# Eight-layer graph network on one core: the sum-stage loops of four engines and TensorE's product loop are loaded at the first slot of an instruction fetch block

## The reference

```python
def layer(h, params):
    W, b, g, beta = params
    h = h * norm_out
    agg = jax.ops.segment_sum(h[src], dst, num_segments=n)
    agg = agg * norm_in
    out = agg @ W + b
    out = _layer_norm(out, g, beta)
    out = jax.nn.gelu(out, approximate=False)
    return (out, None)
h, _ = jax.lax.scan(layer, features, (Ws, bs, ln_g, ln_b))
...
x = _layernorm(x + _L0_gnn_ref(x, src, dst, Ws, bs, ln_g, ln_b), axis=-1)
```

## Time and profile before

| | |
|---|---|
| median of 3 runs | 1668.79 us (1665.58 to 1670.16) |
| the profiled execution's own time | 1669.91 us |
| its span from first to last instruction | 1668.2 us |
| granted TensorE clock, mean share | 0.808 |
| rounds of the sum loop over the 8 layers | 32 (3, 3, 3, 3, 3, 4, 5, 8) |
| rounds of PE's product loop | 84 (7, 7, 7, 7, 9, 11, 14, 22) |

### The profile page before, as it was taken

The page is one execution under the profiler, slowest core; times in us unless marked ns, Lnnn a source line. Parts: engine busy times, 40 slices in busy tenths (PEclk is TensorE's granted clock), DMA queues, the critical chain, the costliest instruction groups (busy, mean ns, idle before and its releaser), DMA issues.

```text
span 1668.2 us, 29286 instructions
## 1 busy us (share of the span) xinstructions
PE 1110.4 (67%) x6235; PEld 916.9 (55%) x6235; DVE 880.2 (53%) x2153; ACT 528.1 (32%) x853; POOL 846.9 (51%) x1023
## 2 busy tenths in 40 slices
PE   7665378677596695776776696679956769992000
PEld 7444123666575575656656585667846667882000
DVE  6445577245354372463563274326733226776776
ACT  4132230232332332233333232333323333441444
POOL 1554300545445464455455365445745445765886
PEclk9556559788898897798898898789987889996555
DMA  0930000523514415225225324441244448545998
GB/s 14 377 130 3 2 1 6 159 82 126 158 57 139 133 69 170 78 107 163 71 106 164 107 76 138 139 126 66 91 139 147 149 126 321 189 169 180 312 302 291
DMA packets 98038, 224.52 MB, mean 135 GB/s; under 512 B 14496, under 2 KB 14496, under 8 KB 97968
## 3 DMA queue, kind: packets, MB, share of 16 engines
q0 software_dynamic: 34432, 104.72, 21.2%
q1 hardware_dynamic: 57200, 107.52, 17.9%
q10 hardware_dynamic: 6336, 11.54, 1.9%
HBM read 137.91 MB, written 85.82 MB: 134 GB/s over the span
## 4 chain that ended last, share of the span: by engine, by line
PE 53%; issue 12%; DMA 10%; DVE 8%; POOL 5%; ACT 4%; another core or an unknown queue 3%; ACTq 2%; DVEq 2%; POOLq 0%; SPq 0%
PE ps_a L1200 16%; PE ps_y L1220 9%; PE ps_y L1221 9%; PE ps_y L1225 9%; DMA rows<-h_rows,slot 4%; POOL rows L507 3%; DMA rows<-h_rows,idx_f 2%; PE ps_y L1216 2%; DMA h_rows<-rows 2%; PE ps_a L1115 2%; DVE agg_t L607 2%; PE ps_a L1181 1%; ACT agg_t L958 1%; DVEq L821 1%
## 5 line engine op out<-in xcount | busy, mean ns | idle before, releaser
L1200 PE MATMUL ps_a<-sel,rows 128*128 128x128 f32 x2560 | 407.0, 323 | 278.1 <-DVE sel L789 122.8
L1200 PEld LDWEIGHTS ps_a<-sel,rows 128*128 128x128 f32 x2560 | 377.1, 233 | 309.6 <-issue 309.0
L456 POOL DMA_INDIRECT rows<-h_rows,slot x290 | 279.8, 965 | 258.3 <-issue 124.6
L995 ACT ACTIVATE agg_t<-ps_a 128x508 f32 x320 | 190.7, 596 | 520.7 <-PE ps_a L1200 369.8
L464 POOL TENSOR_TENSOR s_lo<-agg_t,s_hi 128x512 fp32r<-128x512 f32 x168 | 216.9, 1293 | 251.3 <-ACT s_hi L1000 251.3
L789 DVE TENSOR_SCALAR sel<-iota,by_tile 128x128 f32<-128x128 f32 x344 | 126.0, 370 | 395.6 <-PE ps_a L1200 207.2
L1220 PE MATMUL ps_y<-w_hi,s_hi 128*128 128x512 f32 x672 | 268.5, 400 | 10.9 <-ACT s_hi L1000 10.8
L1221 PE MATMUL ps_y<-w_lo,s_hi 128*128 128x512 f32 x672 | 267.6, 398 | 0.0
L1225 PE MATMUL ps_y<-w_hi,s_lo 128*128 128x512 f32 x672 | 183.5, 396 | 0.0
L862 DVE BATCH_NORM_STATS2 small<-ps_y 128x6 f32<-128x512 f32 x168 | 117.3, 698 | 96.1 <-PE ps_y L1225 95.9
L1220 PEld LDWEIGHTS ps_y<-w_hi,s_hi 128*128 128x128 f32 x672 | 129.0, 192 | 42.0 <-issue 15.1
(11 more groups left out here) (210 smaller groups left out, 1268.2 us busy)
## 6 DMA issues: line engine op xcount, KB each, us to landing
h_rows<-rows SPq DMA_DIRECT2D x124, 256.0 KB, 2.0
h_rows<-agg_t SPq DMA_DIRECT2D x1, 20480.0 KB
out<-agg_t SPq DMA_DIRECT2D x78, 256.0 KB
agg_t<-in_x SPq DMA_DIRECT2D x19, 1024.0 KB, 5.7
h_rows<-rows ACTq DMA_DIRECT2D x44, 256.0 KB, 2.3
w_raw<-in_Ws SPq DMA_DIRECT2D x32, 256.0 KB
rows<-h_rows,slot POOLq DMA_INDIRECT x290
rows<-in_ln_g SPq DMA_DIRECT2D x8, 256.0 KB, 3.8
```

The costliest lines, as they stand in the source:

```text
L456: g.indirect_dma_start(out=rows[:, k, :], out_offset=None, in_=table[:, :], in_offset=bass.IndirectOffsetOnAxis(ap=slot[:, k:k + 1], axis=0))\
L995: a.activation(agg_t[:, :, bass.ds(r0 + 1, P - 1)], ps_a[k % GS][:, :, 1:P], ACT.Copy)\
L1200: m = mm(ps_a[k % GS][:, b, :], rows[:, k, b * P:(b + 1) * P], sel[:, k % GS, :], start=True, stop=True)
```

## The change

```diff
+ENG = mybir.EngineType
...
+        def paged(engine, start, end):
+
+            return nc.Fori(start, end, engines=(engine,), head_slot={engine: 0})
...
             def sum_stage(L, table, its, ib):
-                with pool.Fori(0, its) as group:
+                with paged(ENG.Pool, 0, its) as group:
...
                 def tiles(first, end):
-                    with dve.Fori(first, end) as group:
+                    with paged(ENG.DVE, first, end) if end is its else dve.Fori(first, end) as group:
...
-                with act.Fori(0, its) as group:
+                with paged(ENG.Activation, 0, its) as group:
...
             def sum_stage(L, its, ib):
-                with pe.Fori(0, its) as group:
+                with paged(ENG.PE, 0, its) as group:
...
                 pe.wait_ge(b_ok, done(L + 1))
                 pe.sem_inc(pe_tick, 1)
-                with pe.Fori(0, pairs) as pair:
+                with paged(ENG.PE, 0, pairs) as pair:
```

## The result

| | before | after |
|---|---|---|
| median of the runs | 1667.90 us (4 runs, 1665.58 to 1670.16) | 1717.07 us (4 runs, 1709.54 to 1722.05) |
| the profiled execution's own time | 1669.91 us | 1718.0 us |
| ratio | | 1.0296, 95% interval 1.0257 to 1.0334 |

The kernel is 49 us slower.

A forecast was written before the change was run, and what follows sets the result against it. PE bounds the product stages, a chain of waits the sum stages. Profiled 1669.9 us plus 34.5 for stops minus 3 gain gave 1701.4; the runs' median, 1.1 lower, gave 1700.3, stated as 1700, range 1664 to 1725.

The forecast's parts named there:

- Where the chain runs: POOL's and DVE's sum-stage loop entries lie in single file with PE's wait, so delays there count fully.
- Blocks of 128, fetched in their order: POOL, DVE, ACT and SP fetch blocks of 128 instructions in order, PE 256; a target behind a skipped block needs fetching.
- Which entries: Stops at POOL's and DVE's loop entries of layers 1 to 7, 7 each, plus one in layer 0: 15.
- one of the two of layer 0: Allowance of one stop for POOL's and DVE's first entries, which depend on runtime code outside the program.
- The price of a stop: Each on-demand fetch at POOL's or DVE's loop entry stops the engine for 2.3 us.
- the 15 stops: All stops at POOL's and DVE's loop entries: 15 x 2.3 = 34.5 us lost.
- The 4 KB load: The bias load, 2.28 us from issue to DVE's first use, taken as the measure for one stop.
- The upper bound of 3.8: A stop at POOL's or DVE's entry costs at most 3.8 us, as SP's loads of 256 KB.
- What to look for in the profile: POOL's landing-to-gather wait about 3.7 us, DVE's bias-to-selection wait about 3.5, PE's longest wait for rows 13.8.
- The gain of 3 us: DVE's and ACT's loop bodies inside one block save boundary crossings in about half of 32 rounds: about 3 us.
- The lower bound, 0: Least gain from DVE's and ACT's loop bodies lying inside one block: 0 us; the upper bound was 11 us.
- PE and ACT at no cost: PE's and ACT's loop heads lie in the next block and crossings hide behind waits: cost 0.

The follow-up runs named there:

- e4_blocks_of_128: Changed kernel with POOL's, DVE's and ACT's loops placed by multiples of 128 instead of 256, so no block is skipped: 1690.66 us, 1.0074 of the kernel before.
- e7_dve_early: Kernel before, with only DVE's jump to a multiple of 256 added, ahead of its wait for the bias: 1521.28 us, ratio 1.0003.
- e10_dve_two_jumps: Kernel before, with two DVE jumps to multiples of 256, an empty instruction between, ahead of its third-piece loop: 1737.63 us, ratio 1.0339.
- e3_act_pe_only: Kernel before, with only ACT's sum loop and PE's two loops placed as in the change: 1685.05 us, ratio 1.0019.
- e8_both_early: Kernel before, with POOL's jump ahead of its waits for stored rows and DVE's ahead of its bias wait: 1521.05 us, ratio 1.0007.
- e6_pool_two_stops: Kernel before, with two alignments and a semaphore increment between them ahead of POOL's gather loop; only one branch resulted: 1543.53 us, ratio 1.0155.
- e9_two_stops_apart: Kernel before, with two POOL jumps to multiples of 256, an empty instruction between, ahead of its gather loop: 1725.88 us, ratio 1.0264.

## Why the prediction was right

**Where the chain runs.** Right. Both entries stand in single file with PE's wait: the stops cost nothing that can be measured when a wait covers them, and about their full length when none does.

**Blocks of 128, fetched in their order.** Right, and now shown. POOL stops where a block of 128 is skipped, and doesn't where none is (e4_blocks_of_128). The packets fit a fetch in order, in which the block jumped over is brought as well: DVE's 362 instructions a layer take 2.83 blocks without placement, and with it three and the one that is jumped over, so 8 x 1.17 = 9 more, as measured (59 against 50). A second jump adds two blocks in each of 8 layers, 16 more, as measured (75). The stops, and the packet inside each of the 14, show that the block behind the one jumped over had not come yet. The prediction held that the trace shows how many packets came and not which; their times, which it left aside, settle it. The queues are told apart as it assumed: the 16.4 KB packets rose only where PE's loops were placed. PE's blocks are of 256 instructions (16,384 bytes), those of POOL, DVE and ACT of 128 (8,192 bytes).

**Which entries.** POOL's and DVE's of layers 1 to 7, and one of the two of layer 0: right to the count. For layer 0 that was luck, since one of two was an allowance without a reason. The one is POOL's (3.71 us); DVE's in layer 0 shows 0.57 us, as much as the entry of the next block in e4_blocks_of_128 (0.54).

**The price of a stop.** This is the term of the sum that was mis-sized: 2.3 us, taken from the bias's landing, where the runs show 2.86 for POOL and 3.36 for DVE (without the jump's own few hundredths, gaps of 2.56 to 3.03 and of 2.97 to 3.47). Over the 15 stops it is 46.9 us, 3.13 each, instead of 34.5. The 4 KB load was a poor stand-in: in the stop of the third layer POOL waits 1.03 us until the packet starts, 0.46 us for the packet, and 1.07 us more before it goes on. The upper bound of 3.8 held for the mean, though single stops go beyond it (4.06 us in e7_dve_early, 5.0 in e10_dve_two_jumps). What to look for in the profile was right in kind, short in size for the same reason: 3.99 us where 3.7 stood, 4.64 where 3.5 stood, 14.9 where 13.8 stood.

**The gain of 3 us.** Not seen. e3_act_pe_only, which has it for ACT, is at 1.0019 and e8_both_early at 1.0007. The lower bound, 0, was the better value. The two errors have the same sign: 12.4 us for the stops and 3 us for the gain make up 15.4 of the 17 us by which the time is over 1700. Counted by the layers alone, which lost 51.5 us, 4 us more are missing; the shorter last part hides them.

**PE and ACT at no cost.** Right within what can be measured: 0 to 0.4%.

## What to carry to other kernels

Before code is aligned, count what the alignment jumps over. On POOL and DVE, whose instructions come in packets of 8.2 KB, a branch over a whole block of 128 instructions stopped the engine for 2.56 to 3.47 us here, and a branch to the next block cost 0.4 to 0.5 us. If code has to be aligned, put the jump ahead of a wait that the engine has anyway and that is longer than the stop, and not between a landing and the work that the critical chain needs. A loop across a block boundary was no loss that could be measured here (ACT's and PE's placed alone gave 1.0019), so there was nothing to win by the placement. To tell such a stop from a wait, look for an instruction packet in the gap: each of the 14 stops had one. A gap with a packet may still be a wait, since POOL's, DVE's and ACT's packets come by the same queue (q14 rose to 62, 59 and 56 with the loops of each placed).

## What the runs showed of the hardware that I had not expected

- The stop is longer than a 4 KB load takes from issue to use (2.28 us): 2.56 to 3.03 us on POOL, 2.97 to 3.47 on DVE. Other traffic doesn't seem to be the reason: in the double jumps POOL's second stop, with nothing but instruction packets beside it, took 2.96 us, and DVE's second in the third layer, with 43 packets instead of 220 in the first, took 3.50 us after 3.64.
- Two stops in a row don't overlap: 3.17 and 2.96 us on POOL, 3.64 and 3.50 on DVE.
- The entry of the next block, for which no packet comes in between, costs some 0.4 us on POOL and 0.5 on DVE, and that is enough to be measured when it is put on the chain at 15 places (0.74% in all, with ACT's and PE's part and 2 us that no run explains).
- A semaphore increment written between two alignments doesn't keep them apart: in e6_pool_two_stops it stands on the alignment's own line (L319) in POOL's records, with a single branch behind it. An empty instruction did, in e9_two_stops_apart (two branches, at 535.09 and 538.29 us).
